# Second attention stage: scores computed twice, row minima fed back as two contraction rows, sums from pairs added on GpSimd

## What is computed

```python
q, k, v = (qkv[:, :, i].transpose(0, 2, 1, 3) for i in range(3))
attn = softmax(einsum('bhqd,bhkd->bhqk', q, k) * hd ** -0.5, axis=-1)
o = einsum('bhqk,bhkd->bhqd', attn, v).transpose(0, 2, 1, 3).reshape(B, T, D)
```

## Time and profile before

| | us |
|---|---|
| median of 3 runs | 4012.81 (4012.68 to 4015.76) |
| the profiled execution, its own time | 4011.16 |
| its span (first to last instruction) | 4009.4 |

### The profile page before, as it was taken

The page is one execution under the profiler, slowest core; times in us unless marked ns, Lnnn a source line. Parts: engine busy times, 40 slices in busy tenths (PEclk is TensorE's granted clock), DMA queues, the critical chain, the costliest instruction groups (busy, mean ns, idle before and its releaser), DMA issues. The chain is left out here.

```text
span 4009.4 us, 70221 instructions
## 1 busy us (share of the span) xinstructions
PE 3775.5 (94%) x26756; PEld 2543.0 (63%) x26756; DVE 2721.6 (68%) x4863; ACT 2687.9 (67%) x4667; POOL 1035.5 (26%) x1544
## 2 busy tenths in 40 slices
PE   8997999999999986999999959799999999995999
PEld 7885666666666664778888835466666666662555
DVE  4335888888888876444421148688888888885987
ACT  2226888888888854222222238688888888884998
POOL 0004555555555465000000037100000000002554
PEclk9998999999999998999999979899999999997999
DMA  5446233333333088244531038733332333313221
GB/s 189 184 164 152 62 67 62 67 62 67 62 67 62 14 285 272 100 137 158 176 114 53 32 131 303 205 62 67 62 67 62 67 61 67 62 30 127 77 80 51
DMA packets 307567, 419.53 MB, mean 105 GB/s; under 512 B 89449, under 2 KB 165741, under 8 KB 307227
## 3 DMA queue, kind: packets, MB, share of 16 engines
q1 hardware_dynamic: 307232, 415.03, 36.8%
HBM read 257.34 MB, written 157.32 MB: 103 GB/s over the span
## 5 line engine op out<-in xcount | busy, mean ns | idle before, releaser
L555 ACT ACTIVATE Sn<-Sn,mn 128x1024 f32<-128x1024 f32 x1024 | 1174.8, 1147 | 30.4 <-DVE mn L583 19.0
L521 PEld LDWEIGHTS pt<-ident,Sn 128*128 128x128 f32 x8192 | 881.2, 141 | 420.8 <-issue 413.5
L521 PE MATMUL pt<-ident,Sn 128*128 128x128 f32 x8192 | 1123.4, 280 | 1.0 <-DVE PT L547 0.4
L545 ACT ACTIVATE PT<-pt 128x512 f32<-128x512 f32 x1280 | 738.2, 597 | 236.0 <-PE pt L521 235.9
L489 PE MATMUL sp<-KS,QS 97*128 97x512 f32 (+1 forms) x2048 | 733.6, 440 | 45.3 <-DMA KS<-s_khi 23.6
L583 DVE CUSTOM_DVE_ANT_0 Sn<-sp,biastile 128x1024 f32<-128x1024 f32 x512 | 624.4, 1220 | 145.1 <-PE sp L489 113.5
L585 DVE TENSOR_SCALAR_CACHE_REDUCE Sn<-sp 128x1024 f32<-128x1024 f32 x512 | 624.3, 1220 | 137.3 <-PE sp L489 137.3
L628 POOL TENSOR_SCALAR biastile<-dist,ascale 128x1024 f32<-128x1024 f32 x512 | 576.3, 1126 | 497.0 <-DVE mn L583 483.9
L510 PE MATMUL po<-PT,Vp 128*32 128x256 f32 x8192 | 651.4, 391 | 0.0
L547 DVE COPY PT<-pt 128x512 f32<-128x512 f32 x768 | 531.2, 692 | 118.5 <-PE pt L521 118.3
L1077 ACT ACTIVATE gf<-pf,b1T 128x512 f32<-128x512 f32 x128 | 88.3, 690 | 535.4 <-PE pf L1022 530.5
(11 more groups left out here) (237 smaller groups left out, 4985.8 us busy)
## 6 DMA issues: line engine op xcount, KB each, us to landing
QS<-s_qhi SPq DMA_DIRECT2D x128, 256.0 KB, 5.0
KS<-s_khi SPq DMA_DIRECT2D x128, 256.0 KB, 7.2
KS<-s_klo SPq DMA_DIRECT2D x64, 256.0 KB, 6.1
QS<-s_qlo SPq DMA_DIRECT2D x64, 256.0 KB, 6.9
Vp<-s_v SPq DMA_DIRECT2D x64, 256.0 KB, 7.8
s_o<-og SPq DMA_DIRECT2D x32, 512.0 KB, 8.7
xA<-in_x SPq DMA_DIRECT2D x8, 1024.0 KB, 5.7
s_qhi<-qstage SPq DMA_DIRECT2D x32, 256.0 KB, 2.0
```

Of the source, the lines that this page charges most:

```text
L521: op = nc.tensor.transpose(ps[:, i, :], sn[:, (g * HALF + i) * P:(g * HALF + i + 1) * P], K.ident[:])
L545: nc.scalar.activation(dst, src, ACT.Copy).then_inc(*s_cp_act.up())
L555: nc.scalar.activation(sn[:], sn[:], ACT.Exp, scale=-1.0, bias=mn[n % 3][:, t:t + 1], accum_out=sums[n % 5][:, t:t + 1]).then_inc(*s_exp.up())
```

## The change

`stage_attention(K, 1)` becomes `stage_attention1(K)`. The transposes of the exponentials and their 1024 copies out of PSUM go. In their place the scores are computed a second time with the keys on the partitions, after the minima of the head are known, so that the exponentials come out already in the layout that the product with v wants.

For every head: (1) `score` computes all eight tiles as before, and DVE only reduces each to its row minima (`minimum`, a `tensor_reduce` from PSUM, no copy). (2) `minima_halves` splits the 128 x 8 minima into a high and a low fp32r part. (3) `minima_to_rows` turns them, with eight products against the identity, into two rows of 1024 at partitions 96 and 97 of PSUM; ACT copies these into rows 96 and 97 of the q tile. The same rows of the k tiles hold -1, set by POOL once. (4) `score_turned` computes 128 keys x 512 queries over 98 rows, so the minimum is already subtracted, into a PSUM ring of two single banks, one for each half of the queries. (5) ACT takes the exponential of each half straight from PSUM into `PT` (128 x 512, no bias operand, no accumulator). (6) POOL adds the two key tiles of a pair (`two`), and `total` multiplies the sum with ones, four column groups, to give the softmax sums in the same form as the output. (7) `turn_output` transposes both (four transposes per head instead of two), and DVE divides.

The loop now runs over pairs of tiles `w` (256 of them and a tail of 14). The second scores lag the first by 12 tiles (`L_T`), the product with v by 14, the sums by 16. The ring `ps_r` of two tiles serves the scores, the rows of minima and the turned outputs. The diff, cut to its core (semaphores, buffers and the loads are shortened; loads are as before, three pairs deep, and released by the second scores):

```diff
+def stage_attention1(K):
+    ROWS = 3 * HD
+    L_T, L_V, L_S = 12, 14, 16
+    NW = N_TILES // 2
...
+        pT = [S.sb(f"PT1{i}", [P, LT, L]) for i in range(2)]
+        two = [S.sb(f"two1{i}", [P, L]) for i in range(3)]
...
+        ps_r = S.ps_ring("s1", 2, [P, L])
+        pst_r = S.ps_ring("st1", 2, [P, BLK])
+        po, psum = S.ps("po1", [P, QW]), S.ps("psum1", [P, QW])
...
+        def score_turned(u):
...
+            pe.wait_ge(s_row, n + 1)
+            pe.wait_ge(s_neg, 1)
+            for g in range(L // BLK):
+                ps = pst_r.take(pe, (u, g), (s_exp, 2 * u + g + 1))
+                nc.tensor.matmul(ps[:], ks[0:ROWS + 2, j, kb * P:(kb + 1) * P], qs[0:ROWS + 2, j, g * BLK:(g + 1) * BLK],
+                                 start=True, stop=True).then_inc(*s_st.up())
+
+        def minima_to_rows(n):
+            ps = ps_r.take(pe, ("row", n), (s_row, n + 1))
+            pe.wait_ge(s_mm, n + 1)
+            for t in range(LT):
+                op = nc.tensor.matmul(ps[ROWS:ROWS + 2, t * P:(t + 1) * P], mm[n % 2][:, t, :].bitcast(F32), K.ident[:], start=True, stop=True)
+            op.then_inc(*s_mrow.up())
+
+        def times_v(u):
...
+            pe.wait_ge(s_exp, 2 * u + 2)
+            if kb == 0:
+                pe.wait_ge(s_ov, n)
...
+        def total(w):
+            n, k = divmod(w, LT // 2)
+            pe.wait_ge(s_two, w + 1)
+            if k == 0:
+                pe.wait_ge(s_os, n)
+            for g in range(4):
+                op = nc.tensor.matmul(psum[g * HD:(g + 1) * HD, :], K.ones[:, 0:HD], two[w % 3][:, g * QW:(g + 1) * QW],
+                                      start=k == 0, stop=k == LT // 2 - 1)
+            op.then_inc(*s_sum.up())
...
+        def tensor_program():
+            for w in range(NW + 14):
+                u = 2 * w
+                if u < N_TILES:
+                    score(u)
+                if 0 <= u - L_T < N_TILES:
+                    score_turned(u - L_T)
+                n, k = divmod(w - 13, 4)
+                if k == 0 and 0 <= n < N_HEADS:
+                    turn_output(n)
+                for x in (u - L_V, u - L_V + 1):
+                    if 0 <= x < N_TILES:
+                        times_v(x)
+                if 0 <= w - L_S // 2 < NW:
+                    total(w - L_S // 2)
+                n, k = divmod(w - 4, 4)
+                if k == 0 and 0 <= n < N_HEADS:
+                    minima_to_rows(n)
+                if u < N_TILES:
+                    score(u + 1)
+                if 0 <= u - L_T < N_TILES:
+                    score_turned(u - L_T + 1)
...
+        def scalar_program():
+            for w in range(NW + 14):
+                x = 2 * w - L_T
+                for g in range(2):
+                    if 0 <= x < N_TILES:
+                        exponential(x, g)
+                n, k = divmod(w - 11, 4)
+                if k == 0 and 0 <= n < N_HEADS:
...
+                    nc.scalar.activation(ov[n % 2][:, 0, :], po[:], ACT.Copy).then_inc(*s_ov.up())
+                n, k = divmod(w - 12, 4)
+                if k == 0 and 0 <= n < N_HEADS:
...
+                    nc.scalar.activation(ov[n % 2][:, 1, :], psum[:], ACT.Copy).then_inc(*s_os.up())
+                n, k = divmod(w - 4, 4)
+                if k == 0 and 0 <= n < N_HEADS:
...
+                    nc.scalar.activation(qs_l.at[p][0][ROWS:ROWS + 2, j, :], ps_r.at["row", n][ROWS:ROWS + 2, :], ACT.Copy).then_inc(*s_row.up())
+                for g in range(2):
+                    if 0 <= x < N_TILES:
+                        exponential(x + 1, g)
...
+        def minimum(u):
...
+            nc.vector.tensor_reduce(mn[n % 2][:, t:t + 1], ps_r.at["score", u][:], AX.X, ALU.min).then_inc(*s_min.up())
...
+        def gpsimd_program():
...
+            for w in range(NW):
+                n, k = divmod(w, LT // 2)
+                pool.wait_ge(s_exp, 4 * (w + 1))
+                if w >= 3:
+                    pool.wait_ge(s_sum, w - 2)
+                nc.gpsimd.tensor_tensor(two[w % 3][:], pT[n % 2][:, 2 * k, :], pT[n % 2][:, 2 * k + 1, :], ALU.add).then_inc(*s_two.up())
...
-        stage_attention(K, 1)
+        stage_attention1(K)
```

132 lines of the change are left out of this document (added).

## The result

The changed kernel takes 4263.2 us (median of 4, 4260.7 to 4266.7), the kernel before 4012.7 on the same chip: a ratio of 1.062 (95% interval 1.061 to 1.064), 250 us slower. The forecast was 4203, in a range of 4065 to 4290. The profiled execution spans 4258.9 us against 4009.4. T1 runs from 2553.5, the first scores, to 3882.9, the last output: 1329.4 us against 1075.4, 254 more. The other stages together are 4.5 us shorter. One execution of e1 further down ran at a lower granted clock (0.65, 5488 us) and is left out of its time.

A forecast was written before the change was run, and what follows sets the result against it. PE bounds T1 and gains waits on ACT: with these a head takes 19.51 us, 64 heads 1249; with filling T1 is 1265 against 1075, +190, giving 4203 us; range 4065 to 4290.

The forecast's parts named there:

- rival three: ACT's exponential costs 0.690 us instead of 0.597, adding 48 us, result 4251; chance 10%.
- PE's own work: PE's products for a pair of tiles plus one change of mode, without waits: 3.48 us, against 4.12 before.
- The ring's wait: Once per pair, score_turned waits for the exponentials that free its two PSUM banks: 0.52 us, making a pair 4.00.
- Rivals one and two: One: PE never waits for ACT, 3985, 5%. Two: only the ring's wait is hidden, 4070, 10%.
- The copy of `po`: Once per head, times_v waits for ACT's copy of the old po, queued behind two exponentials: 1.09 us.
- The products for the minima: PE's minima_to_rows, eight plain fp32 products of two instructions each, 16 x 0.109 = 1.74 us per head.
- Rival four: Weight loads of minima_to_rows are not hidden: 109 us more, result 4312; chance 8%.
- Rivals three and six: Three: exponential of 0.690 us, 4251, 10%. Six: POOL bounds, its sum taking over 4.0 us, 4560, 2%.
- The copy of the minima: ACT's copy of the two rows of minima holds a slot of ps_r; PE loses 0.03 us per head.
- the wait for the sums: In the round after the po copy, total waits for ACT's copy of the sums: 0.20 us per head.
- What stays covered: Step claiming that DVE (11.1 of 19.5 us per head), POOL, ACT and the loads do not bound.
- Rival five: PE's clock falls to 1.2 GHz for a fifth of the stage, adding roughly 205 us, result 4410; chance 3%.

The follow-up runs named there:

- e1: Changed kernel with score_turned before score in the second half of a round, so two scores lie between the products sharing the ring; 4195.6 us.
- e7: Changed kernel with the edits of e1, e2, e4 and e6 together; 3939.3 us, 0.982 of the kernel before.
- e2: Changed kernel with ACT's copies of po and the sums ahead of the exponentials of their round; 4175.8 us.
- e6: Changed kernel with the minima turned by one product instead of eight and laid into their rows by two DMAs from ACT's queue; 4195.4 us.
- e8: Changed kernel with the edits of e6 and e4 together; 4134.5 us.
- e3: Changed kernel with POOL's addition cut to 16 of 1024 columns, leaving the softmax sums out of the work; 4252.1 us.
- e4: Changed kernel with the subtraction for the low part of the minima moved from DVE to POOL, ahead of POOL's addition; 4257.6 us.
- e5: Changed kernel with the edits of e2 and e4 together; 4128.5 us.
- e9: e7 with turn_output moved behind total instead of ahead of times_v; 3912.6 us, 0.975 of the kernel before.

## Why the prediction was right, and where it was short

The sign and most of the size were right: 190 us forecast, 250 measured. The measured 4263 lies outside the forecast's own range of 4160 to 4250. It lies inside the stated one because that was widened to take in rival three, whose condition (an exponential of 0.690 us) did not hold: 0.594 was measured. That the range still holds the result is luck in this sense, the mechanism is not. Step by step:

- PE's own work, 3.48 us for a pair. Right: without the ring's wait e1 and e7 run plain rounds of 3.53 to 3.55, in which 0.05 to 0.07 may be a rest of a wait.
- The ring's wait, 0.52. Right: 4.01 measured, 0.46 of which e1 takes away. Rivals one and two, in which PE doesn't wait for this ring, are out.
- The copy of `po`, 1.09. Right: 5.10 in the timeline and 4.00 in e2. In every second head it is 5.19; times_v then has a further wait, for the v of a new pair (that this is the cause was not tried).
- The products for the minima, 16 x 0.109 = 1.74. Right to 0.02: the spacing from the rows below is (1.91 - 0.27) / 15 = 0.109, where 0.27 is the recorded duration of one product, and in e6 and e8 14 of them, expected to be 1.53, gave 1.71 together with the copy behind them. Rival four, bare weight loads, is out. Rivals three and six are out by the exponential's 0.594 us and POOL's 2.365.
- The copy of the minima, 0.03 forecast, 0.13 measured as the difference of 3003.89 - 3002.84 = 1.05 (score to next round's score, plain) and 3015.66 - 3014.48 = 1.18 in the long round; the wait for the sums, 0.20 forecast, 3011.71 - 3010.51 - 0.89 = 0.31 measured. Both were mis-sized by about 0.1 us, together 0.21 x 64 = 13 us. The sums' wait has two semaphores, and in the earlier trace rows a release with two waits came 0.12 us after ACT's end (3627.36 to 3627.48), one with a single wait 0.04 (3631.97 to 3632.01); the forecast charged only one. That this is the cause was not tried.
- Missing altogether: the hold of DVE's subtraction by POOL. The step that failed is "What stays covered": it counted how much of the time DVE and POOL work, 11.1 and 10.8 of 19.5 us, and called the reductions and 1.3 us of small work covered. It did not ask whether the two can work at once. Cost 6.68 - 6.21 = 0.47 us per head, 30 us, by e3 and e4.
- The clock. Rival five had a fall to 1.2 GHz at 3%. Small ones came: seven of 3.4 us in the body of T1, 1.6 us each, 11 us. The reason given for leaving it out, that the idle pieces are about 1 us, doesn't hold.

13 + 30 + 11 = 54 us, of the 64 by which T1 was longer than forecast (1329.4 against 1265). The wait in every second head, 0.09 x 32 = 3 us, is a part of the rest; what is left is 0.01 to 0.02 us on several terms of a head and about 2 us of filling and draining. The kernel as a whole is only 60 over, since the other stages came out 4.5 us shorter, which is no merit of the forecast. Of its signs, PE busy for about 85% of T1 failed: it is recorded busy for 1224.77 of 1334 us, 92%, since a product's record covers short waits. The PE timeline of the long round has all but the clock in it:

```profile
3010.51 1.07 PE L734 MATMUL po<-PT,Vp 128*32 128x256 f32 x16
3011.71 0.64 PE L744 MATMUL psum<-two,ones 128*32 128x256 f32 x8
3012.64 1.91 PE L723 MATMUL s<-ident,mm 128*2 128x128 f32 x16 [0.30 <-DVE mm L828]
3014.48 0.73 PE L704 MATMUL s<-KS,QS 96*128 96x512 f32 x2
3015.05 0.62 PE L716 MATMUL st<-QS,KS 98*128 98x512 f32 x2
3015.66 0.73 PE L704 MATMUL s<-KS,QS 96*128 96x512 f32 x2
```

total starts 1.20 behind times_v where 0.89 is its pace (3002.30 - 3001.41 in the plain round); the minima start 0.93 behind total where 0.45 would do (3007.94 - 3007.49 in e5); then 1.84 until the next score.

## What to carry to other kernels

Counting what each engine must do said that this change could gain 28 us (rival one's 3985); walking one round in the order of the queues said that it loses 190, and was right to within 0.1 us in three of four rounds. So where a change shortens the work of the bounding engine but ties it to a ring that another engine frees, lay out one round in time, and look at what stands ahead of each release in the other engine's queue: moving ACT's two copies ahead of two exponentials was worth 87 us, moving one product call 68. And when two engines can't be in use together, their shares of busy time say nothing about that.

## What had not been expected of the hardware

- A DVE instruction on 8 columns was held for 2.3 us by a POOL addition of 2.36 us; which of two small instructions is held depends on when they are issued (the subtraction in the changed kernel, the cast for 1.60 us in e1).
- The clock of PE fell to 0.50 for 3.4 us, 2 to 22 times in the body of T1 (the changed kernel, e3, e4, e6, e8), though in the changed kernel PE was recorded busy for 93% of the time and its longest idle time was 1.0 to 1.4 us. Every fall began within 0.9 us of where times_v resumed after that idle time. There was none where that idle time was gone (e2, e5, e7, e9), and none in e1, where it was 1.3 us but the ring's waits just ahead of it were gone or small. A fall slowed times_v from 1.07 to 1.93 us:

```profile
3105.81 0.98 PE L716 MATMUL st<-QS,KS 98*128 98x512 f32 x2
3107.91 1.93 PE L734 MATMUL po<-PT,Vp 128*32 128x256 f32 x16 [1.12 <-ACT ov L799]
3109.59 1.11 PE L744 MATMUL psum<-two,ones 128*32 128x256 f32 x8
```

  Why some heads caught one and most didn't, and why e6 had 2 and e4 had 22, stays open.
- Plain fp32 products of 128 columns are 0.109 us apart for a weight of two columns, as the prediction had found for the transposes, whose weight has 128: between these two the columns of the weight made no difference.
